# Attention by turns, a latent stage by pairs of items, and a context loaded a second time with features on the partitions

## The chip, the cores and the metric

The program runs on one core of one Trainium2 chip. The metric is the device time of one execution in microseconds (us); lower is better. The engines are named as in the profile: PE (matrix products; PEld is its loading of weights), DVE, ACT, POOL and SP, which only issues DMAs here.

## The reference

The input is x, 32 items of 128 rows by 128 features, and ctx, 32 items of 128 rows by 256 features. The network has five attention layers, each with a feed-forward part behind it. What the change touches:

```
L0..L4 attention:  o = softmax(q k^T * scale + mask) v per head (8 or 16 heads);
                   with L1, L3, L4 a product with w_o and a residual addition behind it
cross (before L3): q  = layernorm(x) @ W_tgt.T + b_tgt
                   kv = (ctx @ W_src.T + b_src) * mask        [128 x 256 per item]
                   x += the part of W_out that meets the target rows
latent (before L4): latent = layernorm(x @ Wdkv.T)            [128 x 64 per item]
                   k = rope(latent @ Wuk.T), v = latent @ Wuv.T
L2 feed-forward ("bit"): weights rounded to -1, 0, 1 times a scale; three-tap convolution
experts (end):     four experts, each row of x through the one that its gate picks
```

A product on PE sums over the partitions. So rows by features have to be turned to features by rows before they meet a weight matrix.

## The kernel before

**Stages.** The program is a row of stages: preparation with L0 attention, feed-forward 0, depooling, routing, gathering, L1 attention (4 tiles), expansion, L2 attention, the bit stage, the cross stage, L3 attention, the latent stage, L4 attention and the experts. Each stage gives every engine a function of its own (`cross_tensor` is PE's part of the cross stage, `_vector` DVE's, `_scalar` ACT's, `_gpsimd` POOL's) and ends in `phase_end`, where every engine drains and waits until all five have come there. Nothing of a later stage starts before.

**Order within a stage.** `steps` (L40) is a software pipeline written out: an engine has a list of (lag, function) pairs, and in step t it does each function for item t minus lag, in the order of the list. `wait_reuse` makes it wait until a buffer that has `depth` copies is free again. Each engine executes its instructions in the order that comes out of this.

**Cross stage.** Per item b, PE turns the normalised row (`turn_rows`, L982), then both 128-wide halves of the context (`turn_ctx`, L1586), then makes the queries (a product of a bias row with ones, L1594, and one 128x128x256 product, L1595), then keys and values (bias L1601, two products L1603). DVE copies the turned context from PSUM to `probs` (`take_ctx`, L1562), normalises the next row and adds the product to x (L1566); ACT takes the turned row, the keys (`take_kv`) and the queries (`take_q`). A float32 product stands in the trace as two or more PE records.

**Latent stage.** In a first part queries and raw latents (128x64 per item) are made. In the second part, per item: ACT scales the latent (`scale`, L1704), PE turns it to 64x128 (`turn_latent`, L1737), ACT copies it to `oT` (`take_turned`, L1711), PE multiplies it with `w_h2` (64x384: keys, rotated keys, values; `keys`, L1743), DVE multiplies keys and rotated keys with cosine and sine (L1661, L1662), POOL adds the two (L1679) and ACT copies the values (`take_v`, L1716).

**Attention.** Per item PE computes the scores twice: raw, so that DVE can take each row's maximum (L380), and once more with the maximum subtracted inside PSUM (product L713 with the turned maximum) for ACT's exponential (L574). PE runs these in two halves of the item: L671 and L703 are the scores, L713 subtracts the maximum, L722 adds the mask. `weighted` (L860) multiplies with v. Between the halves stand the `turns` (L756 to L846), in two parts: `first_part` turns the output o of an earlier item (L800) and q and k of a coming item (L807, L808); `last_part` picks the denominators and outputs of another item (L827). The product of an older item with w_o (L783) and the turn of the maximum (L776) belong to one part or the other, as the table `LOW` (L274) says. DVE takes them out: q times the head mask (`take_qT`, L394), k (`take_kT`, L408), o turned (`take_oT`, L414), the normalised output (`take_o`, L423 and L429), the residual addition (`add_post`, L436) and its statistics (L264). Layers in `LOW` have another order of these and other places in PSUM:

```
        LOW = ("L0", "L2") + ("L3",)
...
                if L not in LOW:
                    first_part()
                    last_part()
                else:
                    last_part()
                    first_part()
```

`weighted` waits for the new maximum (`nmT_ready`) in a layer outside of `LOW`, and for the addition three items back (`x_updated`) in one inside; in both for the normalised output of the item before (`o_scaled`).

**POOL.** In the expansion stage POOL clears pads (L2140 is one of them) and then rounds the weights of the bit stage (`expand_aside`, L2128 to L2133, after the sum `inv_w` is known). In L1 attention it splits maxima and copies v.

Of the kernel before, what the change touches and what calls it, by code (L numbers as in the profile page):

```python
# [21 lines left out]
LATENT = 64  # L22
# [101 lines left out]
def build(nc, t_in, out):  # L124
    with ExitStack() as ctx_:
# [9 lines left out]
        def after(name, n=0):  # L135

            return sem(name), n + begun.get(name, 0)
# [136 lines left out]
        LOW = ("L0", "L2") + ("L3",)  # L274
# [674 lines left out]
        w_h2 = sb("w_h2", [64, 384])  # L949
# [603 lines left out]

        def cross_vector(dve):
# [4 lines left out]
            def take_ctx(b, k):  # L1559
                dve.wait_ge(sem("cr_ctx_turned"), b + 1)  # L1560
                wait_reuse(dve, after("cr_kv"), b, 2)
                nc.vector.tensor_copy(probs[:, k % 2, 0:256], ps[:, 2 + k % 2, 0:256]).then_inc(sem("cr_ctxT"), 1)  # L1562

# [4 lines left out]
            steps(dve, B, [(0, norm_b), (1, take_ctx), (3, add)])  # L1568

        def cross_scalar(act):  # L1570
# [9 lines left out]
            steps(act, B, [(1, take_rows(act)), (3, take_kv), (3, take_q)])  # L1580

        def cross_tensor(pe):
            def turn_ctx(b, k):
                wait_reuse(pe, after("cr_ctxT"), b, 2)
                for c in range(2):
                    last = nc.tensor.transpose(ps[:, 2 + k % 2, 128 * c:128 * c + 128],  # L1586
                                               ctx_all[:, b, 128 * c:128 * c + 128], ident[:])
                last.then_inc(sem("cr_ctx_turned"), 1)

# [7 lines left out]
            def keys(b, k):  # L1597
                pe.wait_ge(sem("cr_ctxT"), b + 1)
# [15 lines left out]
        lat_scale, lat_shift = ctx_all[:, 9, 0:B], ctx_all[:, 9, B:2 * B]  # L1614
        turned_halves = probs[:, 0, 0:1024].rearrange("p (k n) -> p k n", k=RING)

        def latent_vector(dve):
# [39 lines left out]
            def key(b, k):  # L1657
                dve.wait_ge(sem("la_kv"), b + 1)
                wait_reuse(dve, after("la_k"), b, RING)
                half, src = turned_halves[:, k, :], ps[:, 6 + k % 2, :]  # L1660
                V.tensor_tensor(half[:, 0:128], src[:, 0:128], rope[:, 2, :], ALU.mult)  # L1661
                V.tensor_tensor(half[:, 128:256], src[:, 128:256], rope[:, 3, :], ALU.mult  # L1662
                                ).then_inc(sem("la_key_halves"), 1)
            dve.wait_ge(sem("la_q"), B)
            steps(dve, B, [(3, key)])

        def latent_gpsimd(pool):
# [8 lines left out]
            def key(b, k):  # L1676
                pool.wait_ge(sem("la_key_halves"), b + 1)
                half = turned_halves[:, k, :]
                nc.gpsimd.tensor_tensor(kv_all[:, b, 0:128], half[:, 0:128], half[:, 128:256],  # L1679
                                        ALU.add).then_inc(sem("la_k"), 1)  # L1680
            steps(pool, B, [(4, query)])
            steps(pool, B, [(4, key)])

        def latent_scalar(act):
# [17 lines left out]
            def scale(b, k):  # L1702
                wait_reuse(act, after("la_latent_turned"), b, 2)
                nc.scalar.activation(o_sb[:, k % 2, 0:LATENT], lat_raw[:, b, :], ACT.Identity,  # L1704
                                     bias=lat_shift[:, b:b + 1], scale=lat_scale[:, b:b + 1]
                                     ).then_inc(sem("la_latent"), 1)

            def take_turned(b, k):
                act.wait_ge(sem("la_latent_turned"), b + 1)
                wait_reuse(act, after("la_kv"), b, 2)  # L1710
# [633 lines left out]
```

## Time and profile before

| | |
|---|---|
| median of 3 runs | 1465.81 us (1461.55, 1465.81, 1468.51) |
| the profiled execution | 1465.44 us, span 1463.7 us |
| PE busy / PEld | 1306.9 us (89%) / 861.5 us (59%) |
| DVE / ACT / POOL busy | 932.4 / 605.9 / 277.2 us |
| stages, us from the span's start | L1 attention 333 to 391, expansion 391 to 418, bit 545 to 676, cross 676 to 764, L3 attention 764 to 892, latent 894 to 987 (its second part from 923.6), L4 attention 987 to 1194 |

A row of the trace has the start in us, the duration in us, the engine, the source line, the operation, output and inputs, shapes as partitions x elements, and a count where records of one line follow each other. In brackets stands how long the engine was idle before it and what released it. A table by windows has the stretch and its length, then the busy time of each engine with the number of records, the granted TensorE clock as a share of full speed, the busy share of the DMA engines and GB/s.

### The profile page before, as it was taken

How to read it: one execution, taken by the hardware profiler on the slowest of the kernel's cores; microseconds unless marked ns; L12 is line 12 of the kernel's file. 1: busy time of each engine (PE TensorE's matmuls, PEld its weight loads, DVE VectorE, ACT ScalarE, POOL GpSimd, SP SyncE). 2: the span in 40 equal slices, each digit the busy share in tenths (PEclk: the TensorE clock that was granted, in tenths of full speed). 3: DMA queues.
4: the chain of work that ended last, by engine and by line, in shares of the span. 5: the costliest groups of instructions: out<-in, count | busy, mean ns of one | idle time of the engine just before them, and what ended most of it. 6: DMA issues, size and time to landing. Idle time of an engine off the chain costs nothing. (4 is left out here: it accounts for less than half of the span.)

```text
span 1463.7 us, 37014 instructions
## 1 busy us (share of the span) xinstructions
PE 1306.9 (89%) x13899; PEld 861.5 (59%) x13899; DVE 932.4 (64%) x2810; ACT 605.9 (41%) x1375; POOL 277.2 (19%) x782
## 2 busy tenths in 40 slices
PE   3999988839759979998999997899999969999998
PEld 2888876635447754444657885337888844444443
DVE  4677749975367858996336886325777744454554
ACT  2788845641326642222443556542444421111111
POOL 0122211310313320000002223222454520000000
PEclk9999998958869989997998998656999979999999
DMA  9400000000000000000000000001000000000000
GB/s 288 121 3 3 3 2 2 2 1 1 2 1 2 3 2 1 1 1 1 1 1 2 3 3 1 1 0 59 3 3 3 3 2 0 15 8 7 7 7 15
DMA packets 26390, 21.31 MB, mean 15 GB/s; under 512 B 5936, under 2 KB 22512, under 8 KB 26224
## 3 DMA queue, kind: packets, MB, share of 16 engines
q1 hardware_dynamic: 25216, 18.87, 4.6%
q8 instruction: 112, 1.84, 0.5%
q14 instruction: 54, 0.44, 0.1%
q10 hardware_dynamic: 1008, 0.16, 0.1%
HBM read 16.93 MB, written 2.10 MB: 13 GB/s over the span
## 5 line engine op out<-in xcount | busy, mean ns | idle before, releaser
L703 PE MATMUL ps<-kT,qTm 32*128 32x128 f32 x3200 | 250.9, 291 | 1.2 <-issue 0.6
L671 PE MATMUL ps<-qTm,kT 32*128 32x512 f32 (+1 forms) x1024 | 249.1, 550 | 1.8 <-ACT probs L574 1.4
L703 PEld LDWEIGHTS ps<-kT,qTm 32*128 32x128 f32 x3200 | 226.1, 202 | 6.9 <-issue 4.2
L1933 PE MATMUL ps<-kv_all,ctx_all 128*128 128x512 f32 x256 | 134.1, 605 | 5.8 <-DVE kv_all L1846 5.8
L1870 ACT ACTIVATE kv_all<-ps,b_col 128x512 f32<-128x512 f32 x64 | 44.0, 687 | 216.5 <-PE ps L1911 216.5
L1911 PE MATMUL ps<-q_all,ctx_all 128*128 128x512 f32 x256 | 132.4, 600 | 0.0
L380 DVE TENSOR_REDUCE neg_max<-ps 128x8 f32<-128x1024 f32 x72 | 87.7, 1219 | 67.6 <-PE ps L703 67.3
L574 ACT ACTIVATE probs<-ps 128x1024 f32<-128x1024 f32 x72 | 73.8, 1024 | 119.7 <-PE ps L713 119.7
L860 PE MATMUL ps<-probs,v_wide 128*32 128x128 f32 x3200 | 115.2, 277 | 8.5 <-DVE o_sb L429 3.7
L1846 DVE TENSOR_SCALAR kv_all<-ps,b_col 128x512 f32<-128x512 f32 x64 | 48.0, 750 | 116.4 <-PE ps L1911 116.4
L671 PEld LDWEIGHTS ps<-qTm,kT 32*128 32x128 f32 x1024 | 85.2, 189 | 47.9 <-issue 38.8
L499 POOL CAST nm<-neg_max 128x16 bf16<-128x16 f32 (+1 forms) x132 | 27.0, 204 | 426.2 <-DVE neg_max L367 158.2
L375 DVE TENSOR_REDUCE neg_max<-ps 128x4 f32<-128x512 f32 x128 | 82.1, 683 | 34.2 <-PE ps L703 34.1
L394 DVE TENSOR_TENSOR qTm<-ps,hmask 128x512 f32<-128x512 f32 (+1 forms) x132 | 73.4, 556 | 38.4 <-ACT nmT L552 19.7
L570 ACT ACTIVATE probs<-ps,bias_col 128x512 f32<-128x512 f32 x128 | 81.1, 684 | 36.2 <-PE ps L713 36.2
L713 PE MATMUL ps<-nmT,sel_max 32*128 32x128 bf16 x1600 | 95.6, 218 | 0.0
L860 PEld LDWEIGHTS ps<-probs,v_wide 128*32 128x32 f32 x3200 | 80.7, 109 | 24.3 <-issue 13.9
L1529 PE MATMUL ps<-tap_w,xqT 128*128 128x512 f32 x192 | 93.6, 624 | 0.0
L1911 PEld LDWEIGHTS ps<-q_all,ctx_all 128*128 128x128 f32 x256 | 49.1, 192 | 61.3 <-issue 61.3
L564 ACT ACTIVATE probs<-ps,bias_col 128x1024 f32<-128x1024 f32 x64 | 71.4, 1115 | 32.1 <-PE ps L713 32.1
L827 PE MATMUL ps<-pv_pick,pv 128*128 128x72 f32 (+1 forms) x528 | 82.6, 279 | 1.0 <-ACT pv L580 0.9
L580 ACT ACTIVATE pv<-ps 128x256 f32<-128x256 f32 x132 | 50.7, 384 | 72.1 <-PE ps L860 69.6
(379 smaller groups left out, 2703.8 us busy)
## 6 DMA issues: line engine op xcount, KB each, us to landing
ctx_all<-in_ctx SPq DMA_DIRECT2D x4, 1024.0 KB, 10.5
x_all<-in_x SPq DMA_DIRECT2D x4, 512.0 KB, 7.1
out<-x_all SPq DMA_DIRECT2D x8, 256.0 KB, 2.3
ctx_all<-in_W1T SPq DMA_DIRECT2D x1, 1024.0 KB, 5.5
tap_w<-in_conv_wT SPq DMA_DIRECT2D x1, 768.0 KB, 6.9
w_l<-in_w SPq DMA_DIRECT2D x2, 256.0 KB, 3.7
above<-in_c_above SPq DMA_DIRECT2D x1, 256.0 KB, 3.4
rope<-in_c_rope SPq DMA_DIRECT2D x1, 256.0 KB, 2.7
```

What stands on the lines that cost most here:

```text
L375: nc.vector.tensor_reduce(neg_max[:, k, per * g:per * g + per], ps[:, raw_bank(L, b, g), 0:N].rearrange("p (h k) -> p h k", h=per), AX.X, ...
L380: nc.vector.tensor_reduce(neg_max[:, k, H2 * u:H2 * u + H2].rearrange("p (a h) -> p a h", a=2), ps[:, 4 * u:4 * u + 2, 0:N].rearrange("p a ...
L570: nc.scalar.activation(probs[:, k % 2, N * g:N * (g + 1)], ps[:, final_bank(L, b, g), 0:N], ACT.Exp, bias=bias).then_inc(sem("probs_ready" ...
L574: nc.scalar.activation(probs[:, k % 2, 2 * N * u:2 * N * (u + 1)].rearrange("p (a n) -> p a n", a=2), ps[:, 2:4, 0:N], ACT.Exp, bias=bias) ...
L671: nc.tensor.matmul(ps[:, bank, at:at + N], kT[rows_of(g), k, :], qTm[rows_of(g), k, 0:N], start=True, stop=False, skip_group_check=True)
L703: last = nc.tensor.matmul(dst, qTm[rows_of(g), k, 128 * i:128 * i + 128], kT[rows_of(g), k, :], start=False, stop=True, skip_group_check=True)
L713: last = nc.tensor.matmul(dst, sel_max[rows_of(g), i, :], nmT[rows_of(g), k, :], start=False, stop=True, skip_group_check=True)
L827: last = nc.tensor.matmul(ps[:, 7, 256 + W * half:256 + W * half + W], pv[:, k % 2, 128 * half:128 * half + 128], pv_pick[:, 0 if heads == ...
L860: last = nc.tensor.matmul(ps[32 * j:32 * j + 32, 7, 128 * half:128 * half + 128], v_tile(k % 2, heads, 4 * half + j, i), probs[:, k % 2, 1 ...
L1529: last = nc.tensor.matmul(dst, xqT[:, k % 2, tap:tap + 128], tap_w[:, tap, :], start=False, stop=tap == 2)
L1911: nc.tensor.matmul(ps[:, c % 2, :], w_up[:, c, :], xm_T[:, k, :], start=True, stop=True).then_inc(sem("mo_hidden"), 1)
L1933: nc.tensor.matmul(ps[:, 4 + e % 2, :], w_down[:, c, :], hid[:, c % 4, :], start=c % 4 == 0, stop=c % 4 == 3).then_inc(sem("mo_down"), 1)
```

## The change

Four parts.

1. **L4 attention joins `LOW`.** PE does `last_part` ahead of `first_part`; the product (L783) moves to the former, the turn of the maximum (L776) to the end of the latter; DVE takes o and adds right behind its first maximum; `turned_max` and `product_at` take their places of the low layout.
2. **Cross stage.** The host gives ctx a second time as [256, 32, 128]. In the bit stage SP issues two DMAs (4 MB in all) that overwrite `ctx_all` with features on the partitions, each partition one run of 16 KB. The 64 turns of the context (L1586) and the 32 copies (L1562) are gone; PE makes the keys at lag 1, ahead of the queries at lag 2, and ACT takes them at lag 2.
3. **Latent stage, second part, by 16 pairs.** The latents of two items stand side by side, one 128x128 turn serves both, one ACT copy takes it out. The two items' products have 64 rows each, rows 0 to 63 and 64 to 127 of PE, into two PSUM banks; `w_h2` is loaded twice for that (five small loads more in the preparation). DVE has one operation of 512 elements for four of 128, POOL one addition of 256 for two, ACT one copy of the values for two. PSUM holds three pairs.
4. **Rounding of the bit weights** moves from POOL's part of the expansion to the end of its part of L1 attention.

```diff
-        LOW = ("L0", "L2") + ("L3",)
+        LOW = ("L0", "L2") + ("L3", "L4")
...
+        def context_by_feature(sp):
+            for c in range(2):
+                sp.dma_start(ctxT[:, c, :, :], t_in["ctxT"][128 * c:128 * c + 128]).then_inc(sem("ctxT_loaded"), 16)
...
-            steps(dve, B, [(0, norm_b), (1, take_ctx), (3, add)])
+            steps(dve, B, [(0, norm_b), (3, add)])
...
-            steps(act, B, [(1, take_rows(act)), (3, take_kv), (3, take_q)])
+            steps(act, B, [(1, take_rows(act)), (2, take_kv), (3, take_q)])
...
-                pe.wait_ge(sem("cr_ctxT"), b + 1)
+                if b == 0:
+                    pe.wait_ge(sem("ctxT_loaded"), 32)
...
-                    last = nc.tensor.matmul(dst, probs[:, k % 2, 128 * c:128 * c + 128], w_src[:, c, :],
+                    last = nc.tensor.matmul(dst, ctxT[:, c, b, :], w_src[:, c, :],
                                             start=False, stop=c == 1)
...
-            steps(pe, B, [(1, turn_rows(pe)), (1, turn_ctx), (2, queries), (2, keys)])
+            steps(pe, B, [(1, turn_rows(pe)), (1, keys), (2, queries)])
...
+        def pair_banks(p):
+            at = 2 + 2 * (p % 3)
+            return ps[:, at:at + 2, :]
...
+            def take_turned(p, k):
+                act.wait_ge(sem("la_latent_turned"), p + 1)
+                wait_reuse(act, after("la_kv"), p, 2, 2)
+                nc.scalar.activation(oT[:, k % 2, :], ps[:, k % 2, 0:128], ACT.Identity,
+                                     bias=col("ln_b"), scale=col("ln_g")).then_inc(sem("la_latentT"), 1)
...
+            steps(act, PAIRS, [(0, scale), (1, take_turned), (3, take_v)])
...
+            def keys(p, k):
+                pe.wait_ge(sem("la_latentT"), p + 1)
+                wait_reuse(pe, after("la_v"), p, 3)
+                for i in range(2):
+                    rows = slice(LATENT * i, LATENT * i + LATENT)
+                    nc.tensor.matmul(pair_banks(p)[:, i, 0:384], oT[rows, k % 2, :], w_h2[rows, :], start=True,
+                                     stop=True).then_inc(sem("la_kv"), 1)
+            steps(pe, PAIRS, [(1, turn_latents), (2, keys)])
...
-                 gpsimd=lambda e: attention_gpsimd(e, "L1", TILES, 16, False),
+                 gpsimd=lambda e: (attention_gpsimd(e, "L1", TILES, 16, False), round_weights(e)),
...
-            dict(vector=bit_vector, scalar=bit_scalar, tensor=bit_tensor,
+            dict(vector=bit_vector, scalar=bit_scalar, tensor=bit_tensor, sync=context_by_feature,
```

The order of instructions on PE in the cross stage, one item in the middle, before:

```order
L982 MATMUL ps<-ident,row 128x128
L1586 MATMUL ps<-ident,ctx_all 128x128 x2
L1594 MATMUL ps<-bias_rows,onesb 128x256
L1595 MATMUL ps<-w_tgt,rowT 128x256
L1601 MATMUL ps<-bias_rows,onesb 128x256
L1603 MATMUL ps<-w_src,probs 128x256 x2
```

and with the change (line numbers of the changed kernel):

```order
L982 MATMUL ps<-ident,row 128x128
L1596 MATMUL ps<-bias_rows,onesb 128x256
L1598 MATMUL ps<-w_src,ctx_all 128x256 x2
L1588 MATMUL ps<-bias_rows,onesb 128x256
L1589 MATMUL ps<-w_tgt,rowT 128x256
```

The two turns of the context are gone, and the keys' products stand between the turn of the row and the queries.

PE in L4 attention, the second half of one step and the first of the next, with the turns between them, before:

```order
L703 MATMUL ps<-kT,qTm 128x128 x8
L713 MATMUL ps<-nmT,sel_max 128x128 x8
L783 MATMUL ps<-w_o,oT 128x128
L800 MATMUL ps<-ident,o_sb 128x128
L807 MATMUL ps<-ident,q_all 128x128
L808 MATMUL ps<-ident,kv_all 128x128
L776 MATMUL ps<-identb,nm 128x128
L827 MATMUL ps<-pv_pick,pv 128x72 x2
L722 MATMUL ps<-causal,identb 32x512 x8
```

and with the change:

```order
L703 MATMUL ps<-kT,qTm 128x128 x8
L713 MATMUL ps<-nmT,sel_max 128x128 x8
L783 MATMUL ps<-w_o,oT 128x128
L827 MATMUL ps<-pv_pick,pv 128x72 x2
L800 MATMUL ps<-ident,o_sb 128x128
L807 MATMUL ps<-ident,q_all 128x128
L808 MATMUL ps<-ident,kv_all 128x128
L776 MATMUL ps<-identb,nm 128x128
L722 MATMUL ps<-causal,identb 32x512 x8
```

The picking of the outputs (L827) has moved from the end of the turns to their second place. On DVE in L4 attention one item before:

```order
L394 TENSOR_TENSOR qTm<-ps,hmask 128x512
L408 COPY kT<-ps 128x128
L414 COPY oT<-ps 128x128
L423 RECIPROCAL inv_den<-ps 128x16
L429 TENSOR_TENSOR o_sb<-ps,inv_den 128x128
L436 TENSOR_TENSOR ctx_all<-ctx_all,ps 128x128
L264 BN_STATS stats_all<-ctx_all 128x6
L380 TENSOR_REDUCE neg_max<-ps 128x8 x2
```

and with the change:

```order
L423 RECIPROCAL inv_den<-ps 128x16
L429 TENSOR_TENSOR o_sb<-ps,inv_den 128x128
L436 TENSOR_TENSOR ctx_all<-ctx_all,ps 128x128
L264 BN_STATS stats_all<-ctx_all 128x6
L394 TENSOR_TENSOR qTm<-ps,hmask 128x512
L408 COPY kT<-ps 128x128
L414 COPY oT<-ps 128x128
L380 TENSOR_REDUCE neg_max<-ps 128x8 x2
```

The output and the addition (L423 to L264) now stand ahead of the three copies out of the turns (L394 to L414). The counts per item stay what they were.

## Rows read from the trace of the kernel before

**Rows 1.** Busy time by windows: cross stage, latent keys, first part of L4 attention.

```profile
676.00:764.00 88.00, 83.37 (x353) 52.22 (x354) 30.73 (x109) 32.76 (x98) 0.20 (x2) 0.92 0.00 1
923.60:987.00 63.40, 61.38 (x96) 20.24 (x96) 15.62 (x64) 30.64 (x97) 14.52 (x32) 0.50 0.00 1
987.00:1011.00 24.00, 22.69 (x217) 16.42 (x217) 11.47 (x15) 4.42 (x7) 3.91 (x10) 0.50 0.28 89
```

**Rows 2.** Timeline of PE in the cross stage, one item.

```profile
718.24 1.13 PE L1603 MATMUL ps<-w_src,probs 128*128 128x256 f32 x4
719.21 0.27 PE L982 MATMUL ps<-ident,row 128*128 128x128 f32 x1
719.32 0.38 PE L1586 MATMUL ps<-ident,ctx_all 128*128 128x128 f32 x2
719.63 0.28 PE L1594 MATMUL ps<-bias_rows,onesb 3*128 3x256 bf16 x1
719.84 0.70 PE L1595 MATMUL ps<-w_tgt,rowT 128*128 128x256 f32 x2
720.47 0.28 PE L1601 MATMUL ps<-bias_rows,onesb 3*128 3x256 bf16 x1
```

**Rows 3.** The same at half clock: the turn of the row, two successive items.

```profile
684.79 0.42 PE L982 MATMUL ps<-ident,row 128*128 128x128 f32 x1
...
689.23 0.42 PE L982 MATMUL ps<-ident,row 128*128 128x128 f32 x1
```

**Rows 4.** Latent keys: PE's timeline over one item, then groups by line.

```profile
929.02 1.65 PE L1743 MATMUL ps<-w_h,oT 64*128 64x384 f32 x2
930.59 0.42 PE L1737 MATMUL ps<-ident,o_sb 128*64 128x128 f32 x1
930.94 1.01 PE L1743 MATMUL ps<-w_h,oT 64*128 64x384 f32 x1
...
L1711 ACT ACTIVATE oT<-ps,cols 64x128 f32<-64x128 f32 x32 | 14.5, 454 | 30.1 <-PE ps L1737 30.1
L1704 ACT ACTIVATE o_sb<-ctx_all 128x64 f32<-128x64 f32 x32 | 13.7, 431 | 1.6 <-DVEq L1655 1.6
```

**Rows 5.** Timeline of L4: score products on separate 32-row tiles of PE.

```profile
1100.40 0.59 PE L671 MATMUL ps<-qTm,kT 32*128 32x512 f32 x2
```

**Rows 6.** Timeline of L4 at full clock, around two weighted products.

```profile
1098.52 1.08 PE L860 MATMUL ps<-probs,v_wide 128*32 128x128 f32 x32
...
1103.66 0.29 DVE L429 TENSOR_TENSOR o_sb<-ps,inv_den 128x128 f32<-128x128 f32 x1
1103.70 0.39 PE L713 MATMUL ps<-nmT,sel_max 32*128 32x128 bf16 x8
...
1104.20 1.08 PE L860 MATMUL ps<-probs,v_wide 128*32 128x128 f32 x32
...
1177.09 0.39 PE L713 MATMUL ps<-nmT,sel_max 32*128 32x128 bf16 x8
1177.40 1.08 PE L860 MATMUL ps<-probs,v_wide 128*32 128x128 f32 x32
```

**Rows 7.** Timeline of L4 at half clock: one turn in two successive items.

```profile
1002.92 0.47 PE L807 MATMUL ps<-ident,q_all 128*128 128x128 f32 x1
...
1010.34 0.47 PE L807 MATMUL ps<-ident,q_all 128*128 128x128 f32 x1
```

**Rows 8.** Timeline around the start of the expansion, and DVE in L1.

```profile
384.62 0.86 DVE L448 SCALAR_TENSOR_TENSOR x_all<-q_all,place_keep,x_all 128x128 f32<-128x128 f32 x3
...
390.52 1.19 POOL L2140 MEMSET v_wide<- 128x1312 f32 x1 [15.94 <-SPq L971]
...
401.31 3.97 POOL L2133 TENSOR_TENSOR tap_w<-k_pad,tap_w 128x512 f32<-128x512 f32 x3
```

**Rows 9.** DMA: the context's first load, and one small load.

```profile
ctx_all<-in_ctx SPq DMA_DIRECT2D x4, 1024.0 KB, 10.5
...
53.06 0.54 SPq L2022 DMA_DIRECT2D w_h<-in_WukT  x1
```

More of the change, by code:

```diff
@@ L948, in build @@
         w_h1 = sb("w_h1", [128, 320])
[L949 removed]
+        w_h2 = sb("w_h2", [128, 384])
         w_o3 = sb("w_o3", [128, 128])
@@ L1579, in take_kv @@
                                      scale=mask_f[:, bass.ts(b, 1)]).then_inc(sem("cr_kv_taken"), 1)
-            steps(act, B, [(1, take_rows(act)), (3, take_kv), (3, take_q)])
+            steps(act, B, [(1, take_rows(act)), (2, take_kv), (3, take_q)])
         def cross_tensor(pe):
[L1583 to L1588, printed above, removed]
             def queries(b, k):
@@ L1655, in latent_vector, with key @@
             dve.sem_inc(sem("la_scaled"), 1)
[L1657 to L1662, printed above, removed]
+            def key(p, k):
+                dve.wait_ge(sem("la_kv"), 2 * p + 2)
+                wait_reuse(dve, after("la_k"), p, RING)
+                wide = rope[:, 2:4, :].rearrange("p r n -> p (r n)").unsqueeze(1).broadcast_to([128, 2, 256])
+                V.tensor_tensor(pair_halves[:, k, :, :], pair_banks(p)[:, :, 0:256], wide, ALU.mult
                                 ).then_inc(sem("la_key_halves"), 1)
             dve.wait_ge(sem("la_q"), B)
-            steps(dve, B, [(3, key)])
+            steps(dve, PAIRS, [(3, key)])
         def latent_gpsimd(pool):
@@ L1732, in latent_tensor, with turn_latents @@
             pe.wait_ge(sem("la_raw"), B)
-            def turn_latent(b, k):
-                pe.wait_ge(sem("la_latent"), b + 1)
-                wait_reuse(pe, after("la_latentT"), b, 2)
-                nc.tensor.transpose(ps[0:LATENT, 4 + k % 2, 0:128], o_sb[:, k % 2, 0:LATENT],
-                                    ident[:]).then_inc(sem("la_latent_turned"), 1)
-            def keys(b, k):
-                pe.wait_ge(sem("la_latentT"), b + 1)
-                wait_reuse(pe, after("la_v"), b, 2)
-                nc.tensor.matmul(ps[:, 6 + k % 2, 0:384], oT[0:LATENT, k % 2, :], w_h2[:], start=True,
-                                 stop=True).then_inc(sem("la_kv"), 1)
-            steps(pe, B, [(1, turn_latent), (2, keys)])
+            def turn_latents(p, k):
+                pe.wait_ge(sem("la_latent"), 2 * p + 2)
+                wait_reuse(pe, after("la_latentT"), p, 2)
+                nc.tensor.transpose(ps[:, k % 2, 0:128], o_sb[:, k % 2, :], ident[:]).then_inc(sem("la_latent_turned"), 1)
+            def keys(p, k):
[6 more added lines that the diff above has]
+            steps(pe, PAIRS, [(1, turn_latents), (2, keys)])
         GROUPS = B // 4
@@ L1999, in build @@
             (rw_row[:], t_in["router_w"].rearrange("d one -> (one d)").partition_broadcast(128)),
+        ] + [(w_h2[64 * i:64 * i + 64, 128 * c:128 * c + 128], t_in[w])
+             for i in range(2) for c, w in enumerate(("WukT", "WukT_turned", "WuvT"))
+        ] + [(col(n)[64:128, :], t_in[n].rearrange("(s one) -> s one", one=1)) for n in ("ln_g", "ln_b")
         ] + [(col(n, t_in[n].shape[0]), t_in[n].rearrange("(s one) -> s one", one=1))
```

49 lines of the change are left out of this document (21 added, 28 removed).

## The prediction, made before the changed kernel ran

> **What bounds the kernel now.** I read the busy times by windows first, then PE's timeline inside each stage that the change touches. Stages end in a meeting of all engines, so each can be costed by itself. In the cross stage PE is busy 83.37 of 88.00 us, in the latent keys 61.38 of 63.40 [rows 1]: PE bounds both, and neither DVE (30.73 and 15.62) nor ACT (32.76 and 30.64) is near. The granted clock differs: 0.92 in the cross stage, 0.50 (1.2 GHz) in the whole of the latent keys, 0.50 still in the first 24 us of L4 attention [rows 1]. So an instruction on PE in the latent part costs about twice what it does elsewhere. The sum below is made against the profiled execution, 1465.44 us, which stands 0.4 us under the median.
>
> **Cross stage.** At full clock an item takes 720.68 - 718.24 = 2.44 us, where the last product starts 0.21 after its bias, as L1595 does after L1594 (720.47 + 0.21 = 720.68) [rows 2]. Of it: products L1603 0.97 up to the turn of the row, so one 256-column product is 0.485; the row's turn 0.11; the two turns of the context and what stands between them and the bias 0.31; bias 0.21; L1595 0.63; bias 0.21. L1595 has the length of a product and 0.14 more, ahead of a bf16 bias; the turns' 0.31 is two turns at 0.11 and 0.09 more in the same place. This extra at the change from float32 to bf16 thus comes twice per item, and in the new order twice too: turn of the row to bias, and second context product to bias. New item: 0.11 + 0.10, bias 0.21, two products 0.97 + 0.12, bias 0.21, one product 0.485 with a turn behind it: 2.2 us. That is 0.24 less, 32 x 0.24 = 7.7. The stretch at half clock, where an item takes 689.23 - 684.79 = 4.44 [rows 3], gives about twice per item for its three or four items: another 0.6. Taken: **-8**. Bounds: if the copies' removal helps nothing else, 32 x 0.22 (two turns at 0.11) = -7.0; if the extra is gone as well, 32 x 0.45 = -14 cannot be passed. DVE's 32 copies go with no effect on the path: PE is 95% busy. ACT takes the keys one step earlier and DVE adds at the same lag: both have more than half of the item idle.
>
> The new loads: the first load of the context took four DMAs of 1 MB with 10.5 us each to landing [rows 9]. Issued at the start of a bit stage of 131 us in which the DMA queues are empty, 4 MB are covered eleven times over by the first load's own pace (4 x 10.5 = 42 us even end to end). Cost nothing; if the cover were gone, up to 42. The five small loads add five issues of 0.54 us on SP [rows 9] at 53 us from the start, where SP serves L0 attention and nobody waits for these weights until later: nothing.
>
> **Latent keys.** An item is 930.59 - 929.02 = 1.57 for the product and 930.94 - 930.59 = 0.35 for the turn, 1.92 us; 32 of them are 61.6 of the 63.4 us [rows 4, 1]. After it a pair needs one turn and two products that sit on different 64-row halves of PE. The nearest rows for such products are the raw scores of L4, on different 32-row tiles. A float32 product is two records (four L1603 for two products) and takes 0.485 us for 256 columns [rows 2], so two records of 512 columns in series would be 0.97; they end within 0.59 [rows 5]. So tiles of rows run beside each other. Taken: a pair is 1.57, plus 0.2 for the second product's later start, plus 0.35, say 2.1 us. ACT's part per pair is two scalings (431 ns), one copy out (454) and one copy of values, no longer than another 0.45: under 1.8 [rows 4], just below PE. The chain turn, copy (0.45), product of one pair spans steps and overlaps. First step and last step in which PE stands idle: 3.7 us in all (lead 1.9, tail 1.8, the lengths of one old item each). 16 x 2.1 + 3.7 = 37.3 against 63.4: **-26**. Bounds: if both halves ran after one another, 16 x (2 x 1.57 + 0.35) + 3.7 = 59.5, -4; if the clock came up with the denser PE, a pair is bound by ACT's 1.75, 31.7, -32. The row is nearest to the first value: the clock was 0.50 there with PE 97% busy [rows 1], and the new PE has no more work to show.
>
> **L4 attention.** At full clock the weighted product starts every 1104.20 - 1098.52 = 5.68 us. It starts 0.50 after L713; in the drain at the end, with less on DVE, the same step is 1177.40 - 1177.09 = 0.31 [rows 6]. The 0.19 is a wait: DVE's o_sb (L429) ends at 1103.66 + 0.29 = 1103.95, and `weighted` needs it. In the new order DVE makes it ahead of the three copies (L394 to L414), with some 0.9 us to spare, and the addition too. What is late next: q masked for the next item (L394), which now waits until ACT has taken the turned maximum, with the copies of k and o queued behind it on DVE; they are used a step later, so there are some 5 us of slack. 28 items: 28 x 0.19 = **-5.3**. PE does the same work in another order, DVE too. Bounds: 0 if the wait passes to q and k, -7 if half-clock items gain as well.
>
> **Rounding of weights.** In the expansion POOL starts at 390.52 after 15.94 us of idleness, and its rounding ends at 401.31 + 3.97 = 405.28 [rows 8]; the stage lasts until 418, by DVE. So POOL was not what the stage ended by. Moved, some 13.5 us of POOL start at 390.52 - 15.94 = 374.6 and end near 388, under 2 us before L1 attention ends: covered, narrowly. A gain of 0.4 from DVE's small operations that no longer meet POOL's; a loss where POOL and DVE's additions with two SBUF inputs (three of 0.86 us in all, at 384.62 [rows 8]) get in each other's way. I take **+0.5**, bounds -0.5 and +4.
>
> The Trainium skill bears on that last one ("SBUF - State Buffer", section "Who interferes with whom"): DVE and GpSimd share a port pair under an exclusive lock, and a DVE instruction with both inputs in SBUF contends with a GpSimd one. By that rule the rounding, all of it SBUF, and DVE's additions would exclude each other, and the stage would grow by some us; it is rival P. No row of the trace before shows the two together.
>
> **Sum.** -8 - 26 - 5.3 + 0.5 = -38.8; 1465.4 - 38.8 = **1427 us**.
>
> **Rivals.**
> *W, more clock.* For: L4's start and the cross stage's start both have PE at half clock, although busy (22.69 of 24.00 us [rows 1]); what comes ahead of them changes. If the latent keys get full clock, 6 us more; if the cross stage rises earlier, up to 4. Against: nothing in the latent part kept the clock down by being idle. 1465.4 - 38.8 - 9 = 1418.
> The Trainium skill ("TensorE: Matmul & The Clock Gate", "Part 4: PE-mode transpose") says that transposes do not count as activity for the clock; by this rule a cross stage without context turns and a latent stage with half of its turns would rise sooner. That the latent keys, 0.50 with a turn only 0.35 of each 1.92 us [rows 4], did not rise speaks neither for nor strongly against it.
> *S, no overlap of the halves.* The two 64-row products share `oT`'s banks and follow each other in the queue; each brings its own weights, which in [rows 5] was also so and did no harm. Price: 59.5 - 37.3 = 22: 1449.
> *P, POOL's rounding and DVE in each other's way* in L1 attention: +4 against +0.5: 1431.
> *D, DVE or the turned maximum bounds L4.* If q masked came too late, each item would wait for the turn of the maximum (0.11, as L982 [rows 2]), ACT's copy of it (0.45 at most, as L1711 [rows 4]), DVE's mask (0.3, as L429 [rows 6]) and the three handovers (about 0.1 each): 1.2 us for 28 items, +34 in place of -5.3: about 1466, no change. Against: the slack of 5 us.
> *K, the clock stays down, slower.* L4 attention starts at half clock, where an item takes 1010.34 - 1002.92 = 7.42 [rows 7], 1.74 more than at full clock. PE arrives there out of a latent stage with more idle time per item than before. If it never rises in L4, 28 x 1.74 = 49 is lost against the 38.8 gained: 1475. It is even with before at 22 such items, and slower by over 0.5% from 27 on. Against: four or five slow items were enough before.
>
> **Chances.** A, the forecast: 0.60. W 0.14, S 0.11, P 0.08, D 0.03, K 0.04. The range takes A with its bounds (cross -7 to -10, latents -24 to -28, L4 -2 to -7), P, and W: 1412 to 1440; S, D and K, 0.18, stay out. A change of 0.5% is 7.3 us, about what a measurement of this kernel can tell from no change: faster are A, W, S and P, 0.93; D is 0.03; slower K, 0.04.
>
> **What would show it.** Cross stage: L1586 gone, L1603's successor at 2.2 us per item, stage about 80 us. Latent keys: both halves' products starting within 0.3 us of one another, a period of 2.1 us, 37 us in all, clock still 0.50. L4: 0.31 from L713 to L860, period 5.5. L1 attention no longer by more than 1 us. It is wrong if the two products of a pair start 1.5 us apart (S), if the period of L4 is still 5.68, if the clock in L4 rises after more than five items (K), or if ACT, not PE, ends the pair.

## The result, and the profile after

The changed kernel takes 1416.37 us (median of 4 runs, 1414.12 to 1418.31), the kernel before 1466.18 (4 runs, 1461.55 to 1468.51). The ratio is 0.9664, interval 0.9636 to 0.9691: 49.8 us faster. Forecast were 38.8 and 1427 us, range 1412 to 1440. The profiled execution took 1416.78 us, its span is 1414.9.

Each engine but SP works in nearly every stage, so SP's drain, which comes at once where SP has nothing to do, dates the start of a stage. For L4 attention it is SP's first expert load, and for the end of L4 ACT's last table load and junk operation.

| stage | before | after | difference | forecast |
|---|---|---|---|---|
| L1 attention and expansion | 57.0 + 28.5 | 57.5 + 27.5 | -0.5 | +0.5 |
| cross | 87.2 | 77.1 | -10.1 | -8 |
| L3 attention | 128.2 | 128.3 | +0.1 | 0 |
| latent | 95.0 | 56.7 | -38.3 | -26 |
| L4 attention | 204.6 | 202.0 | -2.6 | -5.3 |
| experts | 272.1 | 271.7 | -0.4 | 0 |
| the rest | | | +2.9 | 0 |
| span | 1463.7 | 1414.9 | -48.8 | -38.8 |

The rest is work that the change doesn't touch: L2 attention took 121.9 for 119.3 us and the gathering 23.6 for 22.2, both with a later rise of the clock, L0 attention 1.3 less. The start of L0 attention to the end of the gathering differs in this way from profile to profile, also between kernels that are the same up to there. L2 attention does not: it comes back with the rounding below.

The busy times by windows of the changed kernel (columns as in [rows 1]), first the cross stage's first 24 us, then latent keys, then L4 attention in pieces:

```profile
679.10:703.10 24.00, 20.89 (x77) 12.35 (x78) 7.08 (x29) 7.64 (x26) 0.00 (x0) 0.84 0.00 1
915.90:941.10 25.20, 22.27 (x80) 8.13 (x80) 11.02 (x16) 21.75 (x65) 11.55 (x16) 0.81 0.00 1
961.00:971.00 10.00, 9.35 (x132) 7.26 (x128) 3.96 (x5) 3.31 (x5) 4.52 (x9) 0.55 0.01 2
1125.00:1143.00 18.00, 12.43 (x158) 8.46 (x158) 6.01 (x25) 5.70 (x9) 4.61 (x5) 0.84 0.00 1
```

The latent keys take 25.2 us for the 63.4 of [rows 1], and their clock is 0.81 where it was 0.50. L4 attention is still at half clock in most of 961 to 971 (0.55), that is 20 to 30 us behind its start at 941.17. PE's timeline of the changed kernel shows one item of the cross stage (it answers to [rows 2]):

```profile
716.67 0.27 PE L982 MATMUL ps<-ident,row 128*128 128x128 f32 x1
716.88 0.28 PE L1596 MATMUL ps<-bias_rows,onesb 3*128 3x256 bf16 x1
717.08 1.13 PE L1598 MATMUL ps<-w_src,ctx_all 128*128 128x256 f32 x4
718.15 0.28 PE L1588 MATMUL ps<-bias_rows,onesb 3*128 3x256 bf16 x1
718.36 0.70 PE L1589 MATMUL ps<-w_tgt,rowT 128*128 128x256 f32 x2
718.89 0.27 PE L982 MATMUL ps<-ident,row 128*128 128x128 f32 x1
```

From turn to turn 2.22 us: 2.2 was the forecast. The same view in the latent keys, PE over the pairs where the clock rises (it answers to [rows 4]), and ACT once it is up:

```profile
921.86 1.65 PE L1748 MATMUL ps<-w_h,oT 64*128 64x384 f32 x4
923.44 0.48 PE L1741 MATMUL ps<-ident,o_sb 128*128 128x128 f32 x1
923.84 1.65 PE L1748 MATMUL ps<-w_h,oT 64*128 64x384 f32 x4
925.42 0.36 PE L1741 MATMUL ps<-ident,o_sb 128*128 128x128 f32 x1
925.72 0.92 PE L1748 MATMUL ps<-w_h,oT 64*128 64x384 f32 x4
926.56 0.33 PE L1741 MATMUL ps<-ident,o_sb 128*128 128x128 f32 x1
...
929.77 0.45 ACT L1715 ACTIVATE oT<-ps,cols 128x128 f32<-128x128 f32 x1
930.11 0.38 ACT L1720 ACTIVATE kv_all<-ps 128x256 f32<-128x256 f32 x1
930.38 0.78 ACT L1708 ACTIVATE o_sb<-ctx_all 128x64 f32<-128x64 f32 x2
931.04 0.46 ACT L1715 ACTIVATE oT<-ps,cols 128x128 f32<-128x128 f32 x1
```

Four records (two products) take 1.65 us at half clock, as long as one product did: the halves of PE work beside each other. A pair is 923.84 - 921.86 = 1.98 us at half clock. At full clock PE makes it in 1.14 (925.42 to 926.56), but ACT's four operations follow one another without a gap in 931.04 - 929.77 = 1.27: ACT is the bound then, which was one of the prediction's signs of being wrong. Both are less than was reckoned (2.1, and 1.75 for ACT, whose operations start 0.26 to 0.34 us behind one another though each is listed with 0.4).

L4 attention at full clock (it answers to [rows 6]):

```profile
1050.07 0.39 PE L713 MATMUL ps<-nmT,sel_max 32*128 32x128 bf16 x8
1050.38 1.08 PE L860 MATMUL ps<-probs,v_wide 128*32 128x128 f32 x32
...
1055.84 1.08 PE L860 MATMUL ps<-probs,v_wide 128*32 128x128 f32 x32
...
1054.55 0.29 DVE L429 TENSOR_TENSOR o_sb<-ps,inv_den 128x128 f32<-128x128 f32 x1
```

L713 to L860 is 0.31 as forecast, the period 1055.84 - 1050.38 = 5.46 for 5.68, and the output is ready 1.0 us ahead of its use. Why the stage still gave only 2.6 us is a question for the experiments.

### The profile page after: what moved, and what is told of

It is laid out like the page before. It is cut to its first block and busy times, and to the rows that moved or that the text cites. A ratio compares the mean times of both kernels' runs of the same rounds, so it can differ in the third digit from the quotient of the medians.

```text
span 1414.9 us, 36612 instructions
## 1 busy us (share of the span) xinstructions
PE 1260.0 (89%) x13819; PEld 841.6 (59%) x13819; DVE 919.3 (65%) x2730; ACT 591.5 (42%) x1343; POOL 273.6 (19%) x766
## 5 line engine op out<-in xcount | busy, mean ns | idle before, releaser
L860 PE MATMUL ps<-probs,v_wide 128*32 128x128 f32 x3200 | 116.9, 280 | 4.6 <-DVE o_sb L429 1.7
L499 POOL CAST nm<-neg_max 128x16 bf16<-128x16 f32 (+1 forms) x132 | 26.8, 203 | 428.6 <-DVE neg_max L367 160.9
L394 DVE TENSOR_TENSOR qTm<-ps,hmask 128x512 f32<-128x512 f32 (+1 forms) x132 | 73.2, 555 | 37.7 <-ACT nmT L552 20.6
L713 PE MATMUL ps<-nmT,sel_max 32*128 32x128 bf16 x1600 | 95.9, 219 | 0.0
L860 PEld LDWEIGHTS ps<-probs,v_wide 128*32 128x32 f32 x3200 | 80.8, 111 | 19.6 <-issue 6.5
L827 PE MATMUL ps<-pv_pick,pv 128*128 128x72 f32 (+1 forms) x528 | 82.0, 278 | 0.9 <-ACT pv L580 0.9
```

Of the source, the lines that this page charges most:

```text
L713: last = nc.tensor.matmul(dst, sel_max[rows_of(g), i, :], nmT[rows_of(g), k, :], start=False, stop=True, skip_group_check=True)
L827: last = nc.tensor.matmul(ps[:, 7, 256 + W * half:256 + W * half + W], pv[:, k % 2, 128 * half:128 * half + 128], pv_pick[:, 0 if heads == ...
L860: last = nc.tensor.matmul(ps[32 * j:32 * j + 32, 7, 128 * half:128 * half + 128], v_tile(k % 2, heads, 4 * half + j, i), probs[:, k % 2, 1 ...
```

## The experiments

All times stand against runs of the kernel before of the same chip; the medians of these were 1467.3 (the parts alone), 1464.4 (`e5_serial` to `e8_nolow`), 1467.1 (`e9_fill` to `e11_split`) and 1467.2 us (`e12_best`). Gains by the medians and by the ratios differ by up to 2 us; stages are read from one profiled execution of each kernel. No kernel leaves work out; several do more than they need.

**The parts alone.** Each takes one part of the change onto the kernel before. `e1_low` is `LOW = ("L0", "L2") + ("L3", "L4")` and nothing else; `e2_cross` the cross stage with the second load; `e3_pairs` the latent keys; `e4_round` the rounding.

> Only the new order of L4 attention. Theory 1 (the order takes away the wait of the weighted product for the normalised output): an item of L4 at full clock 5.45 us as in the profile of the change, 5.68 before; 28 items by 0.23 = -6.4 us, and the clock rises about 25 us after the start of L4, as before. Rival (the order also changes when the clock rises, some 4 us later, as it does in the profile of the change): -6.4 + 2 = about -4.

> Only the context by features in the cross stage. Theory 1 (two turns per item less, and half clock for 5 us less): item 2.22 us at full clock, stage 77 us for 87, together -10 us. Rival (the earlier rise of the clock is chance and not of the change): item 2.22 us but stage 79 to 80, together -7 to -8.

> Only the latent keys by pairs. Theory 1 (shorter work and full clock from about 8 us on): a pair 1.99 us at half clock and 1.27 at full clock, keys part about 26 us for 63, together -37 to -39 us. Rival (full clock in the profile of the change was chance, or owed to the shorter cross stage): keys part 16 x 1.99 + 4 = 36 us, together -27.

> Only the rounding moved. Theory 1: L1 attention +0.5 us and the expansion -0.9, as the stage boundaries of the profile of the change show; together between -0.5 and 0. Rival (POOL and DVE get in each other's way in L1 attention): +2 to +4 us, with DVE's L448 longer than 0.86 us for three.

| | us | ratio, interval | stage |
|---|---|---|---|
| e1_low | 1459.6 (10 runs, 1454.1 to 1462.6) | 0.9947, 0.9931 to 0.9963 | L4 200.8 for 204.6 |
| e2_cross | 1455.6 | 0.9923, 0.9899 to 0.9948 | cross 77.0 for 87.2 |
| e3_pairs | 1422.4 | 0.9696, 0.9672 to 0.9719 | latent 55.0 for 95.0, L4 201.0 |
| e4_round | 1466.8 (12 runs) | 1.0000, 0.9986 to 1.0014 | L1 57.5, expansion 27.6, L2 122.0 for 119.3 |

`e1_low` gained 7.8 us by the medians (5.4 to 10.1 by the interval), more than the 3.8 of its profiled L4 attention and more than either value expected of it; the clock rose 27.7 us behind the stage's start for 24.7 before, as the rival had it. `e2_cross` came out as its first theory had it. The pairs give 44.6 us alone by the ratio, more than 39: 40.0 in the latent stage of their profile and 3.6 in L4 behind it, which was sooner at full clock (below).

The parts don't add up. By the medians they give 65 us one by one and 50 together; by the profiled executions 58 and 49. Of these 9 us, 5 are in L4 attention, whose half-clock stretch was 14 us behind the pairs alone and 27 in the change, and 2 in the latent keys, where the clock rose 8.6 us behind the first turn in the change and 4.9 in e3_pairs. The last 2 to 3 are the rounding, whose loss in L2 attention e4_round's profile makes up by a shorter way to L1 attention.

The rounding gives nothing that can be measured in the total. But it moves the clock of L2 attention. The first 30 us of that stage, before and e4_round:

```profile
419.03:449.03 30.00, 24.80 (x331) 18.60 (x331) 17.40 (x42) 13.21 (x29) 5.70 (x28) 0.68 0.01 2
416.01:446.01 30.00, 25.03 (x277) 18.78 (x277) 15.34 (x37) 11.63 (x26) 4.73 (x24) 0.57 0.01 2
```

0.68 is 19 us at half clock, 0.57 is 26. L2 attention takes 119.2 to 119.3 us in all seven profiles without the moved rounding and 121.9 to 122.1 in all seven with it, although its instructions are the same. So the move loses 2.7 us there, against 0.5 lost in L1 attention and 0.9 gained in the expansion. Why the clock rises later is not shown, and a loss of 2.3 us is as much as e4_round's interval can hide.

The rounding did meet DVE: in e4_round's profile DVE's additions in L1 attention read

```profile
374.69 1.05 DVE L448 SCALAR_TENSOR_TENSOR x_all<-q_all,place_keep,x_all 128x128 f32<-128x128 f32 x3
380.94 3.33 DVE L448 SCALAR_TENSOR_TENSOR x_all<-q_all,place_keep,x_all 128x128 f32<-128x128 f32 x3
385.41 0.86 DVE L448 SCALAR_TENSOR_TENSOR x_all<-q_all,place_keep,x_all 128x128 f32<-128x128 f32 x3
```

where each took 0.86 before [rows 8]: 3.33 while POOL multiplied two inputs out of SBUF (its last three operations, 380.16 to 384.13), 0.86 when POOL was done. The Trainium skill states an exclusive lock for this ("SBUF — State Buffer", "Who interferes with whom"), and these three agree, each as long as one of POOL's. The first three, at 374.69, ran beside a POOL operation with one SBUF input (374.47 to 376.39) and took only 1.05. DVE was not what L1 attention ended by: the stage grew by 0.5 us, 57.5 for 57.0.

**Why does the clock rise in the latent keys?** Three kernels. `e5_serial` is `e3_pairs` with both products over all 128 rows, the other item's 64 weight rows zero:

```diff
-                    rows = slice(LATENT * i, LATENT * i + LATENT)
-                    nc.tensor.matmul(pair_banks(p)[:, i, 0:384], oT[rows, k % 2, :], w_h2[rows, :], start=True,
+                    nc.tensor.matmul(pair_banks(p)[:, i, 0:384], oT[:, k % 2, :], (w_h2, w_h2b)[i][:], start=True,
```

`e6_rows` is the kernel before, item by item, with the same number of instructions in the keys part, but turn and product over 128 rows, 64 of which meet zeros:

```diff
-                nc.tensor.transpose(ps[0:LATENT, 4 + k % 2, 0:128], o_sb[:, k % 2, 0:LATENT],
+                nc.tensor.transpose(ps[:, 4 + k % 2, 0:128], o_sb[:, k % 2, :],
...
-                nc.tensor.matmul(ps[:, 6 + k % 2, 0:384], oT[0:LATENT, k % 2, :], w_h2[:], start=True,
+                nc.tensor.matmul(ps[:, 6 + k % 2, 0:384], oT[:, k % 2, :], w_h2[:], start=True,
```

> The latent keys by pairs alone, but each of a pair's two products over all 128 rows (the weights of the other item's 64 rows are zero), so that they cannot run beside each other on PE. Theory 1 (two things made the gain: products beside each other, and full clock, which comes because all 128 rows work): clock rises, a pair is bound by PE at full clock at 2 x 0.8 + 0.3 = 1.9 us, keys part about 36 us, -28 against before. Rival 1 (the clock rises only because two products run at once): half clock throughout, a pair 2 x 1.57 + 0.41 = 3.5 us, keys part 59 us, -4. Rival 2 (the halves bring nothing, ACT was the bound all along): keys part 26 us as in the alone run of the pairs.

> The kernel before, latent keys per item as there, but turn and product over 128 rows where they had 64 (the weights of the lower 64 rows are zero). Theory 1 (64 of 128 rows keep the clock at half in the keys part): the clock rises within some 10 us; an item is then bound by ACT or PE at about 1.1 us, keys part about 40 us for 63, -23, and L4 may begin with less half clock, another -6. Rival (rows do not matter; the items' rhythm or the turns keep the clock down): 0.50 throughout, item 1.97 us for 1.92, keys part +2.

`e6_rows` takes 1433.0 us (2 runs), 0.9783 (0.9751 to 0.9816), 31 us less than before, with no pairs at all. PE's timeline of it, and its windows:

```profile
926.31 0.42 PE L1737 MATMUL ps<-ident,o_sb 128*128 128x128 f32 x1
926.52 1.49 PE L1743 MATMUL ps<-w_h,oT 128*128 128x384 f32 x2
927.80 0.42 PE L1737 MATMUL ps<-ident,o_sb 128*128 128x128 f32 x1
...
929.75 0.27 PE L1737 MATMUL ps<-ident,o_sb 128*128 128x128 f32 x1
929.96 0.88 PE L1743 MATMUL ps<-w_h,oT 128*128 128x384 f32 x2
930.68 0.27 PE L1737 MATMUL ps<-ident,o_sb 128*128 128x128 f32 x1
...
930.00:940.00 10.00, 9.90 (x33) 4.75 (x33) 5.33 (x22) 9.85 (x33) 4.58 (x11) 1.00 0.01 2
```

Some 6 us after the keys' first turn (922.4) the clock rises and stays, where it was 0.50 for 63.4 us with PE 97% busy [rows 1]. What differs is the rows at work (and that the turn is of 128 columns, not 64). With it went another thing: PE no longer changes between a 128-row and a 64-row instruction. That alone did not keep the clock down, as e3_pairs shows:

```profile
924.19 1.05 PE L1746 MATMUL ps<-ident,o_sb 128*128 128x128 f32 x2 [5.39 <-ACT o_sb L1713]
...
928.76 0.47 PE L1746 MATMUL ps<-ident,o_sb 128*128 128x128 f32 x1
929.16 0.92 PE L1753 MATMUL ps<-w_h,oT 64*128 64x384 f32 x4
```

There PE changes just as often, twice per pair of 1.99 us for twice per item of 1.92, but two products of 64 rows are at work at once, and the clock rose 4.9 us behind the first turn (924.19; the products take 0.92 from 929.16 on). The change seems to have its own price, though: at half clock an item takes 1.49 us in e6_rows for 1.92, although it multiplies twice as many rows. The Trainium skill ("TensorEngine Tiling (Array Packing)", "Key Properties") says that a change of tiling mode drains the engine; 0.43 us for two changes per item agrees, but no run separates it from the rows.

`e5_serial` takes 1428.5 us (2 runs), 0.9753 (0.9720 to 0.9785). Its clock rises too, and a pair is 942.10 - 940.70 = 1.40 us, PE bound. 1.9 was expected: a product takes 0.65 at full clock, not 0.8.

```profile
940.70 0.27 PE L1747 MATMUL ps<-ident,o_sb 128*128 128x128 f32 x1
940.80 0.81 PE L1753 MATMUL ps<-w_h,oT 128*128 128x384 f32 x2
941.45 0.81 PE L1753 MATMUL ps<-w_h2b,oT 128*128 128x384 f32 x2
942.10 0.27 PE L1747 MATMUL ps<-ident,o_sb 128*128 128x128 f32 x1
```

The latent stage takes 95.0 us before, 66.4 in e6_rows, 59.4 in e5_serial and 55.0 in e3_pairs. So of the 40 us, taken in this order, 29 come with 128 rows at work instead of 64, 7 more with the pairs' fewer and wider instructions, and 4 with products beside each other (by the medians of the whole kernel 31, 5 and 9, with L4 attention in them). The order matters: at half clock a pair side by side took 1.98 us for the 3.84 of two items, which is the gain that the forecast counted. With the clock up, a pair takes 1.27 us side by side, bound by ACT, and 1.40 one after the other, so the gain shrinks.

**Why does the cross stage give 10 and not 8?** `e7_turns` is `e2_cross` with two turns per item kept, into a bank that nobody reads.

```diff
+            def turn_idle(b, k):
+                if b == 0:
+                    pe.wait_ge(sem("ctxT_loaded"), 32)
+                for c in range(2):
+                    nc.tensor.transpose(ps[:, 2 + k % 2, 128 * c:128 * c + 128], ctxT[:, c, b, :], ident[:])
...
-            steps(pe, B, [(1, turn_rows(pe)), (1, keys), (2, queries)])
+            steps(pe, B, [(1, turn_rows(pe)), (1, turn_idle), (1, keys), (2, queries)])
```

> The cross stage as in the change alone, but with two turns of 128x128 per item kept on PE, into a bank that nobody reads and nobody waits for. Theory 1 (turns cost their own 0.11 us each, 0.22 to 0.32 per item, and do not move the clock): item 2.45 to 2.54 us, half clock to about 5 us after the first product as without them, -3 to -4 against before. Rival (turns do not count for the clock and delay it): half clock for about 10 us after the first product as before, another +2.4 us: -1. Rival 2 (DVE's copies were part of the path): an item stays near 2.22.

It takes 1461.4 us (10 runs), 0.9979 (0.9960 to 0.9997); an item takes 2.44 us, to the hundredth what it took before, so DVE's 32 copies were off the path:

```profile
720.00 0.27 PE L982 MATMUL ps<-ident,row 128*128 128x128 f32 x1
...
722.44 0.27 PE L982 MATMUL ps<-ident,row 128*128 128x128 f32 x1
```

What the clock does is best read from the first 24 us of the cross stage, here before, e1_low, e7_turns, e2_cross:

```profile
676.60:700.60 24.00, 20.92 (x74) 12.99 (x75) 8.63 (x34) 6.62 (x21) 0.00 (x0) 0.70 0.00 1
677.10:701.10 24.00, 20.91 (x67) 12.66 (x68) 8.27 (x32) 6.02 (x19) 0.00 (x0) 0.63 0.00 0
675.20:699.20 24.00, 20.90 (x80) 13.25 (x81) 6.52 (x27) 6.69 (x23) 0.00 (x0) 0.78 0.00 1
677.00:701.00 24.00, 20.95 (x78) 12.38 (x79) 7.07 (x29) 7.62 (x26) 0.00 (x0) 0.85 0.00 0
```

The six profiles with context turns in the old order (before, e1_low, e3_pairs, e4_round, e5_serial, e6_rows) have 0.63 to 0.70, the six without turns (after, e2_cross, e8_nolow to e11_split) 0.84 or 0.85, e7_turns lies between with 0.78. 0.70 is 14.4 us at half clock, 0.78 is 10.6, 0.85 is 7.2. So the new cross stage is at full clock sooner by 7 us and more, worth over 3 us beside the 32 x 0.22 = 7.0 us that the turns cost themselves. Of this the turns alone bring 3.4 us, from e7_turns to e2_cross. The other 4 and more come with what e7_turns has of the new stage, the order of keys and queries and DVE without its copies; no run parts the two. The gain of 3 us is what the first theory expected, but not by its way: the turns do delay the clock, though by less than the rival had it. The Trainium skill ("TensorE: Matmul & The Clock Gate", "Part 4: PE-mode transpose") says that a transpose doesn't count as PE-busy in the same way; the 3.4 us agree in direction with this.

**Why does L4 give so little?** `e8_nolow` is the whole change without the new order in L4.

> The whole change but for the order of L4 attention. Theory 1 (the old order meets full clock in L4 earlier, 13 us of half clock in place of 27, once the stage before it ran at full clock): stage 0.25 us longer per item at full clock, but 12 us less at half clock: 1410 to 1414 us, no slower than the change. Rival (the short half-clock stretch of the run of the pairs alone was chance): 1422 us, since the wait of 0.23 us per item is back.

1418.7 us (5 runs, 1417.5 to 1423.1), 0.9685 (0.9663 to 0.9707): 2 us above the change, 3 by the ratios, within the uncertainty of both. Theory 1 was wrong: its L4 had a long half-clock stretch too, as long as the change's. That makes the two profiles the fair comparison: L4 attention takes 206.6 us in e8_nolow and 202.0 in the change, so the new order is worth 4.6. The first 32 us of L4 attention in four profiles, before, e3_pairs, e8_nolow, after:

```profile
987.04:1019.04 32.00, 30.48 (x388) 22.57 (x392) 17.18 (x24) 8.37 (x13) 7.81 (x16) 0.61 0.21 67
947.06:979.06 32.00, 29.65 (x452) 22.03 (x452) 18.88 (x26) 10.01 (x16) 9.64 (x21) 0.79 0.22 68
942.56:974.56 32.00, 30.51 (x344) 22.58 (x348) 15.43 (x20) 7.40 (x12) 7.08 (x16) 0.57 0.22 67
941.17:973.17 32.00, 30.42 (x344) 22.53 (x348) 15.60 (x21) 7.41 (x12) 7.10 (x16) 0.57 0.21 67
```

Where the latent stage ends at full clock, the half-clock stretch of L4 differs from kernel to kernel, from 14 us (e3_pairs) to 27 (e8_nolow), with the same instructions; I found no rule for when it ends. Runs of one kernel differ in the same way: of e10_fill's the fastest (1402.1 us) had a mean granted clock of 0.940 and the slowest (1410.9) 0.931, but where in the kernel is not known, since one run of each was profiled. L4 splits into the time to the first weighted product, from there to the last one's last records, and the rest: 25.9 + 173.6 + 5.1 us before, 27.1 + 167.5 + 6.3 in e1_low, 26.8 + 174.8 + 5.1 in e8_nolow, 26.8 + 168.1 + 7.1 after. So the new order gains 5.5 to 6.7 in the middle as forecast. The 1 us at the start is a later rise of the clock. In the change it is not of the order, since e8_nolow has it too; in e1_low it may be, where the clock rose 27.7 us into the stage for 24.3 to 24.7 in the four kernels with the old order and the old latent stage. At the end the order loses 1 to 2 us. Part of this is clock, which is 0.84 in the last 18 us now (row above) and was 1.00 in the last 5 before. But e9_fill (below) takes 6.0 us there at 0.97, so 1 us is of the order itself.

**Can the clock be kept up?** `e9_fill` puts eight idle products behind the last latent product, `e10_fill` also six in each of the first four steps of L4. Their inputs are bf16 constants, nobody reads the results. `e11_split` moves the second scaling of each pair to DVE.

```diff
             steps(pe, PAIRS, [(1, turn_latents), (2, keys)])
+            for _ in range(8):
+                nc.tensor.matmul(ps[:, 0, 0:512], identb[:], causal[:].rearrange("p a b -> p (a b)"), start=True, stop=True)
...
             def turns(items):
+                if L == "L4" and next(iter(items.items()))[1][0] + next(iter(items.items()))[0] - 1 < 4:
+                    for _ in range(6):
+                        nc.tensor.matmul(ps[:, 7, 256:512], identb[:], causal[:, 0:2, :].rearrange("p a b -> p (a b)"),
+                                         start=True, stop=True)
```

> The changed kernel, with eight idle products (128 rows, bf16, 512 columns, results read by nobody) on PE behind its last latent product, so that PE does not stand idle for the 1.8 us before L4 attention. Theory 1 (the idle gap at the stage's end drops the clock): full clock goes on into L4, half-clock stretch of 27 us gone or much shorter, -6 to -13 us against the changed kernel's 1416. Rival (L4's first steps, products over 32 rows, bring the clock down and keep it there by themselves): the clock falls some us later and rises where it did; 1415 to 1417.

> As e9_fill, and six more idle products of 256 columns over 128 rows in each of the first four steps of L4 attention. Theory 1 (few rows at work keep the clock down, as in the latent keys): the clock rises within 10 us of L4's start, where it took 27; -8 us for that, +0.6 x 4 = +3 for the idle products; 1409 to 1412. Rival (rows are not what keeps L4's start down): half clock for 27 us and more, +4 us: 1420.

> The changed kernel, with the second scaling of each pair moved from ACT to DVE. Theory 1 (ACT bounds a pair of latent keys at full clock: 1.27 us = its four operations in series): a pair takes PE's 1.1 us, latent keys -2 us. Rival (PE or the handovers bound it): a pair stays at 1.27 us, no change.

e9_fill: 1410.9 us, 0.9616 (0.9598 to 0.9633); full clock goes on 5 us into L4, then falls to half for 17 us all the same. e10_fill: 1405.5 us (1402.1 to 1410.9), 0.9573 (0.9548 to 0.9598), and the first 32 us of its L4 attention are

```profile
943.34:975.34 32.00, 29.91 (x569) 23.39 (x569) 21.65 (x31) 11.23 (x18) 11.79 (x24) 1.00 0.21 68
```

The clock doesn't fall in these 32 us. L4 takes 194 us for 202, with 24 more products in it. Together the two say: without the idle gap the clock falls later and for less long, and a few 128-row products among the 32-row ones of the first steps hold it up. It is not that they fill PE's time: in the first 4.9 us of L4 PE is busy 3.92 us in e9_fill and 4.07 in e10_fill, and over 32 us 30.42 in the change and 29.91 here. That the added products are bf16 and the stage's own mostly float32 was not tried apart. e11_split: 1412.5 us, 0.9625 (0.9607 to 0.9642); a pair takes 1.11 us (930.44 to 931.55 between turns), PE bound as Theory 1 had it. Its latent stage takes 55.3 us for 56.7; the total is 4 us under the change (6 by the ratios, whose intervals just meet), more than the split explains, and its L4 attention had 24 us of half clock for 27.

**Together.** `e12_best` is e10_fill and e11_split, with 21 idle products of 512 columns between latent queries and latent keys, where PE stood idle for 5.4 us, and 6 at the start of the cross stage.

> The changed kernel with what the runs point to: the second scaling on DVE (as e11_split), the idle products of e10_fill, and more of them on PE where it stands idle: 21 of 512 columns between the latent queries and the latent keys, 6 at the start of the cross stage. Theory 1 (idle gaps and products over few rows are what drops the clock): the latent keys begin at full clock, all pairs at 1.1 us, -3 us, cross up 3 us sooner, -1.5, second scaling -2, against e10_fill's 1405.5: about 1399. Rival (the gap of 5.4 us does not drop the clock, the rhythm of the keys does): keys still half clock for some 8 us, 1403.

1399.9 us (4 runs, 1396.2 to 1404.9), 0.9544 (0.9511 to 0.9577): 67 us less than before, 16 to 18 less than the change, and as expected (1399). The keys now begin at full clock, PE's timeline of their first pairs:

```profile
911.51 3.63 PE L1752 MATMUL ps<-causal,identb 128*128 128x512 bf16 x16
915.52 0.53 PE L1758 MATMUL ps<-ident,o_sb 128*128 128x128 f32 x2 [0.38 <-DVE o_sb L1675]
916.37 0.92 PE L1765 MATMUL ps<-w_h,oT 64*128 64x384 f32 x4 [0.32 <-ACT oT L1727]
917.22 0.33 PE L1758 MATMUL ps<-ident,o_sb 128*128 128x128 f32 x1
```

The cross stage's rise did not come sooner, although 1.5 us had been expected of it: its clock was up 7.5 us behind the stage's start, as in the change's profile.

## Why the prediction was right, and where not

- **Direction and range:** right; 1416.4 lies in 1412 to 1440, 10.6 under the forecast, next to rival W's 1418. It is W's mechanism that came, not the forecast's: the clock in the latent keys, the largest term, was taken wrongly. W's number is close partly by luck: the latent keys and the cross stage gave 14 us more than the sum, not 9, and L4 and L2 attention took 5 of it back.
- **Cross, -8 (was -10.1):** the item's working held, 2.2 against 2.22 us, so 7.0 us and not 7.7. Mis-sized was "gives about twice per item for its three or four items: another 0.6": the half-clock stretch itself became 7 us shorter (the windows of the profiles above), which is worth 3. The rival named it, the sum did not.
- **Loads hidden:** right; the bit stage took 138.4 us from start to end for 138.3 before (it starts at 538.3, not at the 545 of the table ahead of the prediction), with 4 MB under it, and PE waited for nothing at the first keys.
- **Latent, -26 (was -38.3):** the step that failed is "The row is nearest to the first value: the clock was 0.50 there with PE 97% busy [rows 1], and the new PE has no more work to show", and in rival W "nothing in the latent part kept the clock down by being idle". Idleness did not; rows did. e6_rows raised the clock by 128 rows in place of 64 alone, and the keys of the change ran at 0.81. The pair was 2.1 in the sum and 1.98 at half clock, 1.27 at full clock, bound by ACT, for which 1.75 was reckoned because durations in place of distances between starts were added. The side-by-side halves (rival S's question) work as the row of L4 said.
- **L4, -5.3 (was -2.6; 4.6 against e8_nolow, at the same stretch of half clock):** wait named rightly, size in the middle 5.5 to 6.7. Missing were the ends of the stage, where the new order loses 1 to 2 us in the drain and the clock rose later, the latter not by the order.
- **Rounding, +0.5 (was -0.5 in its two stages, alone 0.0 in total):** right for these two stages. Not seen was the stage behind them: L2 attention's clock rises 6 us later in every profile with the moved rounding and costs 2.7. Rival P's mechanism is there, three additions in 3.33 us for 0.86, but its price is wrong, since DVE had slack.
- **Rivals D and K:** neither came. DVE's output has 1 us to spare; L4's half clock lasted until 28.7 us behind its start for 24.7, not endlessly.

## What to carry to other kernels

Where a stage of PE stays at half clock although PE is busy, look at how many of the 128 rows its instructions use before counting instructions: filling the rows, even with zeros, was worth 31 us here, more than the 26 that the pairs were reckoned at at the old clock. A few idle 128-row products, in the gap ahead of a stage and among its 32-row ones, were worth 6 and another 5 us here. Parts that shift each other's clock don't add up: measure them together too. And cost an engine that is to become the bound by the distance between the starts of its operations, not by the sum of their durations.

## What the runs showed of the hardware

- With a float32 product of 64 rows and 384 columns, alternating with a turn that loads 128 rows, the granted clock stayed at 0.50 for 63 us at 97% busy; with 128 rows it rose to 1.00 after some 6 us and an item took 0.93 us in place of 1.92 (e6_rows). With two 64-row products side by side it rose after 4.9 us (e3_pairs) and 8.6 (the change).
- An item of alternating 64-row and 128-row instructions took 0.43 us more at half clock than one of 128-row instructions alone (1.92 against 1.49), though the latter works on more rows.
- Two turns of 128x128 per 2.4 us of products delayed the rise of the clock in the cross stage by 3.4 us (0.78 against 0.85 over 24 us), together with the old order and DVE's copies by 7 or more.
- The same L2 attention was at half clock for 19 us in seven profiles and for 26 in the seven whose rounding on POOL had moved out of the stage before it; the cause is open.
- L4's first steps, products over 32 rows, ran at half clock for 14 to 27 us, differently from kernel to kernel; runs of one kernel differ by 4 to 9 us.
